# Attention sums carried from group to group: a vector add in SBUF, or an identity product into the accumulating bank

## The reference, cut to what matters

```python
alpha = einsum(h_src, a_src) + einsum(h_dst, a_dst) + sum(relu(edge_attr @ edge_W.T + edge_b) * h_dst)
alpha = where(alpha >= 0, alpha, 0.2 * alpha)
amax = segment_max(alpha, dst)
ex = exp(alpha - amax[dst])
denom = segment_sum(ex, dst)
out = segment_sum(h_src * (ex / denom[dst])[..., None], dst)
```

## Time and profile before

| | |
|---|---|
| median of 3 runs | 2690.42 us (2685.27 to 2691.62) |
| profiled execution | 2690.11 us, its span 2688.3 us |
| attention stage | about 1542 to 2216 us |
| busy in the whole span | TensorE 72%, VectorE 62%, GpSimd 46%, ScalarE 34% |
| mean granted TensorE clock | 0.87 |
| DMA | 366 MB, mean 136 GB/s |

### The profile page before, as it was taken

One profiled execution on the slowest core, in us unless ns is written; L12 is line 12 of the kernel. 1 busy time (PEld: TensorE's weight loads), 2 busy tenths in 40 slices (PEclk: granted clock), 3 DMA queues, 4 the chain that ended last, 5 costly groups with the idle time before them and its releaser, 6 DMA issues. The chain is left out here.

```text
span 2688.3 us, 41194 instructions
## 1 busy us (share of the span) xinstructions
PE 1935.6 (72%) x12513; PEld 1495.2 (56%) x12602; DVE 1661.8 (62%) x3351; ACT 908.4 (34%) x2284; POOL 1235.4 (46%) x1222
## 2 busy tenths in 40 slices
PE   3366666666279986599922478888888877969995
PEld 1244545445157765499921256666666652329994
DVE  8556555555157767655566779999999986021222
ACT  7333323333100002133312445555555543413331
POOL 0377777777710000255511377777777740002221
PEclk9678877776689998699966689999999998989997
DMA  2355544444478851522223155555555535001113
GB/s 78 106 181 201 188 165 169 171 162 166 145 284 287 293 190 65 169 72 72 71 87 103 43 173 162 159 161 158 162 163 159 163 90 188 18 2 36 36 38 112
DMA packets 192123, 366.13 MB, mean 136 GB/s; under 512 B 47573, under 2 KB 102632, under 8 KB 191525
## 3 DMA queue, kind: packets, MB, share of 16 engines
q1 hardware_dynamic: 135472, 207.05, 23.8%
q0 software_dynamic: 56160, 156.43, 18.5%
q10 hardware_dynamic: 274, 0.00, 0.0%
HBM read 232.23 MB, written 131.07 MB: 135 GB/s over the span
## 5 line engine op out<-in xcount | busy, mean ns | idle before, releaser
L1930 POOL DMA_INDIRECT att_rows<-hdram,top_ix x488 | 501.7, 1028 | 149.7 <-issue 145.7
L839 POOL DMA_INDIRECT mtab<-first_w,msgs_ix x308 | 309.0, 1003 | 94.0 <-issue 88.5
L708 PE MATMUL msgs_p_m<-nodes_n,msgs_hott 128*128 x976 | 319.8, 484 | 37.9 <-issue 30.7
L2000 PE MATMUL att_p_acc<-att_msg,att_hot 128*128 128x264 f32 x976 | 255.7, 407 | 78.3 <-ACT att_msg L2045 56.2
L708 PEld LDWEIGHTS msgs_p_m<-nodes_n,msgs_hott 128*128 128x128 f32 x976 | 223.7, 241 | 90.3 <-issue 53.4
L2000 PEld LDWEIGHTS att_p_acc<-att_msg,att_hot 128*128 128x128 f32 x976 | 180.9, 195 | 122.7 <-DVE att_msg L2167 57.3
L1141 POOL IOTA route_column<- 128x50 f32 (+1 forms) x2 | 0.3, 172 | 523.7 <-ACTq L1137 523.7
L1341 PE MATMUL exp_y<-exp_own,exp_ht 128*128 128x256 f32 x1032 | 239.0, 379 | 2.4 <-issue 2.4
L2030 ACT ACTIVATE att_enc<-att_p_z 128x1024 f32<-128x1024 f32 x122 | 125.0, 1024 | 301.3 <-PE att_p_z L1943 301.3
L839 POOL DMA_INDIRECT mtab<-msgs_rw,msgs_ix x180 | 181.8, 1010 | 72.8 <-issue 52.8
L1341 PEld LDWEIGHTS exp_y<-exp_own,exp_ht 128*128 128x128 f32 x1032 | 188.5, 190 | 24.7 <-issue 3.1
(11 more groups left out here) (389 smaller groups left out, 3997.9 us busy)
## 6 DMA issues: line engine op xcount, KB each, us to landing
first_w<-mtab SPq DMA_DIRECT2D x77, 520.0 KB, 4.8
etab<-msgs_et SPq DMA_DIRECT2D x122, 288.0 KB, 2.2
att_hz<-etab SPq DMA_DIRECT2D x122, 288.0 KB, 2.9
msgs_rw<-mtab SPq DMA_DIRECT2D x45, 520.0 KB, 4.7
first_w<-in_L_ffn_w SPq DMA_DIRECT2D x16, 512.0 KB, 4.7
ffn0x_w<-in_L_ffn_w SPq DMA_DIRECT2D x16, 512.0 KB
ffn_w<-in_L_ffn_Wd SPq DMA_DIRECT2D x8, 1024.0 KB, 11.8
att_rows<-hdram,top_ix POOLq DMA_INDIRECT x488, 3.0
```

Source lines behind the costliest of these rows:

```text
L708: last = T.matmul(p_m[g % 2][:, q, :], hott[g % 2][:, q, :], node, start=True, stop=True)
L839: nc.gpsimd.indirect_dma_start(mtab, bass.IndirectOffsetOnAxis(ap=ix[:, g, q:q + 1], axis=0), rw[g % RS][:, q, :], None).then_inc(s_free[g ...
L1930: nc.gpsimd.indirect_dma_start(rows[:, g % RS, q, :], None, hdram, bass.IndirectOffsetOnAxis(ap=ix1[:, g, q:q + 1], axis=0)).then_inc(s_ro ...
L2000: last = T.matmul(p_acc[g % 2][:, 0:HW], hot[g % 2][:, q, :], msg[g % 2][:, q, :], start=(q == 0), stop=(q == G - 1))
```

## The change

The running sum no longer goes through VectorE. `sums(g)` keeps its bank open after the four products and adds a fifth: the identity as weights and the tile `total` of group g-1 as moving side, so that the bank holds the group's sums plus the old total. ScalarE then copies the bank out twice: `pass_total(g)` copies it to `total`, scaled by `keep` for group g+1 (for the last group of a batch without scale, since VectorE's `fallen` multiplies it by `fall`, which also holds the change of a tile); and `keep_total(g)` copies it to `acc`. `gathered` is gone. `fallen` runs once per batch, at the end of a step with s % 4 = 3, ahead of `alphas`. `pass_total(s - 8)` stands in ScalarE's step behind `encodings(s + 1)`; `keep_total` keeps its place, for group s - 8 in place of s - 9. The semaphore `s_add` goes; `s_total` and `s_fallen` come.

```diff
--- before.py
+++ after.py
@@ -1888,9 +1888,9 @@
     p_top = a.ps("p_top", [P, 512])
     p_line, p_back, a_top, a_edge = (p_top[:, k * P:(k + 1) * P] for k in range(4))
     (s_z, s_enc, s_h, s_prod, s_red, s_adst, s_al, s_line, s_chain, s_rb, s_back, s_backc, s_top, s_new, s_fall, s_edge,
-     s_dif, s_ex, s_msg, s_wide, s_acc, s_add, s_go, s_weight, s_kept, s_node) = (a.sem(m) for m in (
+     s_dif, s_ex, s_msg, s_wide, s_acc, s_total, s_go, s_weight, s_kept, s_node, s_fallen) = (a.sem(m) for m in (
          "z", "enc", "h", "prod", "red", "adst", "al", "line", "chain", "rb", "back", "backc", "top", "new", "fall", "edge",
-         "dif", "ex", "msg", "wide", "acc", "add", "go", "weight", "kept", "node"))
+         "dif", "ex", "msg", "wide", "acc", "total", "go", "weight", "kept", "node", "fallen"))
     s_rows, s_hz, s_seg = ([a.sem(f"{m}{s}") for s in range(k)] for m, k in (("rows", RS), ("hz", SE), ("seg", 2)))
 
     def groups(t):
@@ -1995,10 +1995,16 @@
                 pe.wait_ge(s_wide, g + 1)
                 pe.wait_ge(s_weight, g + 1)
                 if g >= 2:
-                    pe.wait_ge(s_add, g - 1)
+                    pe.wait_ge(s_kept, g - 1)
                 for q in range(G):
                     last = T.matmul(p_acc[g % 2][:, 0:HW], hot[g % 2][:, q, :], msg[g % 2][:, q, :],
-                                    start=(q == 0), stop=(q == G - 1))
+                                    start=(q == 0), stop=(g == 0 and q == G - 1))
+                if g:
+                    if g % BG == 0:
+                        pe.wait_ge(s_fallen, g // BG)
+                    else:
+                        pe.wait_ge(s_total, g)
+                    last = T.matmul(p_acc[g % 2][:, 0:HW], cst["ident"][:], total[(g - 1) % 2][:], start=False, stop=True)
                 last.then_inc(s_acc, 1)
 
             encoders(0)
@@ -2060,12 +2066,20 @@
                 act.wait_ge(s_new, t + 1)
                 S.activation(fall[t % 2][:], fall[t % 2][:], ACT.Exp).then_inc(s_fall, 1)
 
+            def pass_total(g):
+                act.wait_ge(s_acc, g + 1)
+                if g + 1 < NG:
+                    if (g + 1) % BG:
+                        S.activation(total[g % 2][:], p_acc[g % 2][:, 0:HW], ACT.Copy,
+                                     scale=keep[:, g + 1:g + 2]).then_inc(s_total, 1)
+                    else:
+                        S.copy(total[g % 2][:], p_acc[g % 2][:, 0:HW]).then_inc(s_total, 1)
+
             def keep_total(g):
                 b = act.value_load(gb[0:1, g:g + 1], min_val=0, max_val=NT - 1)
-                act.wait_ge(s_add, g + 1)
                 if g:
                     act.wait_ge(s_kept, g)
-                S.copy(acc[:, bass.ds(b, 1), :].rearrange("p a c -> p (a c)"), total[g % 2][:]).then_inc(s_kept, 1)
+                S.copy(acc[:, bass.ds(b, 1), :].rearrange("p a c -> p (a c)"), p_acc[g % 2][:, 0:HW]).then_inc(s_kept, 1)
 
             def exponents(t):
                 w = len(groups(t)) * G
@@ -2080,6 +2094,8 @@
                 t, j = s // BG, s % BG
                 if s + 1 < NG:
                     encodings(s + 1)
+                if 0 <= s - LAG - 1 < NG:
+                    pass_total(s - LAG - 1)
                 if s + 2 < NG:
                     own_tile(s + 2)
                 if j == 0 and 0 < t <= NB:
@@ -2092,8 +2108,8 @@
                     weights(s - LAG)
                 if 0 < s - LAG + 1 < NG:
                     widen(s - LAG + 1)
-                if 0 <= s - LAG - 2 < NG:
-                    keep_total(s - LAG - 2)
+                if 0 <= s - LAG - 1 < NG:
+                    keep_total(s - LAG - 1)
             act.wait_ge(s_kept, NG)
 
         @block.vector
@@ -2168,26 +2184,15 @@
                                 rows[:, g % RS, :, 0:C].rearrange("p q (h d) -> p q h d", d=D),
                                 bc(ex[t % 2][:, j * G:(j + 1) * G, :], 3, D), ALU.mult).then_inc(s_msg, 1)
 
-            def gathered(g):
-                t, j = g // BG, g % BG
-                last, to = total[(g + 1) % 2], total[g % 2]
-                if g >= 2:
-                    dve.wait_ge(s_kept, g - 1)
-                if j == 0:
-                    dve.wait_ge(s_fall, t + 1)
-                    link(V.tensor_tensor(to[:].rearrange("p (h d) -> p h d", d=D + 1),
-                                         last[:].rearrange("p (h d) -> p h d", d=D + 1), bc(fall[t % 2][:], 2, D + 1), ALU.mult))
-                    dve.wait_ge(s_acc, g + 1)
-                    V.tensor_tensor(to[:], to[:], p_acc[g % 2][:, 0:HW], ALU.add).then_inc(s_add, 1)
-                else:
-                    dve.wait_ge(s_acc, g + 1)
-                    V.scalar_tensor_tensor(to[:], last[:], keep[:, g:g + 1], p_acc[g % 2][:, 0:HW], ALU.mult,
-                                           ALU.add).then_inc(s_add, 1)
-                dve.wait_ge(s_add, g + 1)
+            def fallen(t):
+                to = total[(t * BG - 1) % 2]
+                dve.wait_ge(s_fall, t + 1)
+                dve.wait_ge(s_total, t * BG)
+                V.tensor_tensor(to[:].rearrange("p (h d) -> p h d", d=D + 1), to[:].rearrange("p (h d) -> p h d", d=D + 1),
+                                bc(fall[t % 2][:], 2, D + 1), ALU.mult).then_inc(s_fallen, 1)
 
             same_windows()
             link(V.memset(tops[:, 0, :], -BIG))
-            link(V.memset(total[1][:], 0.0))
             for s in range(NG + LAG + 3):
                 t, j = s // BG, s % BG
                 if s < NG:
@@ -2200,8 +2205,8 @@
                     differences(t - 1)
                 if 0 <= s - LAG < NG:
                     messages(s - LAG)
-                if 0 <= s - LAG - 1 < NG:
-                    gathered(s - LAG - 1)
+                    if (s - LAG) % BG == 0 and s > LAG:
+                        fallen((s - LAG) // BG)
                 if s < NG and (j == BG - 1 or s == NG - 1):
                     alphas(t)
```

## The result

The changed kernel takes 2765.57 us (median of 4 runs, 2764.07 to 2767.94), the kernel before in the same comparison 2690.35: a ratio of 1.0284, 95% interval 1.0266 to 1.0302. It is slower by 75 us; the forecast was 2766.

What follows compares the result with a forecast made beforehand. The prediction took a ring of TensorE and ScalarE waiting for each other, not VectorE, as the bound; +66.2 us in the window, +2.4 before and +7.5 after, together +76 on 2690, gave 2766 us, range 2740 to 2800.

Steps and rivals of the forecast that it cites:

- the ring: Attention loop: TensorE's `p_z`, ScalarE's Relu, `own_tile`, `weights`, TensorE's sums, next `p_z`; 20.50 us per batch, growing to 23.76.
- TensorE's product: The fifth, identity product after each group's four, in every group but the first: 0.467 us, wholly in the ring.
- rival 4: On TensorE the fifth product's wait holds back its weight load: up to 46 us more, 2789 to 2812 us; chance 0.07.
- ScalarE's copy: `pass_total` between Relu and `own_tile`, in the ring: net 0.37 us for three groups of a batch, 0.28 for one.
- rival 3: ScalarE's idle time absorbs the copy, so only TensorE's term counts: about 2724 us; chance 0.04.
- Nothing for `keep_total` and `fallen`: `keep_total`, last in ScalarE's step, and `fallen`, once per batch on VectorE, fit in spare time and cost nothing.
- the last groups: The last eight groups, without Relus between, become a chain with sums about 3.2 us apart: +7.5 us.
- the half-clock steps: Four loop places with TensorE's clock at half level, counted as gone; if they stay, 7 us more or slightly above.
- rival 5: TensorE's longer gap before the sums drops its clock once per batch: 63 us more, 2829 us; chance 0.04.
- 66.2, 2.4 and 7.5: Added us for the 109 full-pipeline steps, the steps before that window, and the last eight groups; together +76.
- GpSimd is the bound: GpSimd's gathers, 5.33 us per group, set the mean step, so nothing moves: 2690 us; chance 0.03.
- the 22.6 us credited for the fourth step: Most that removing VectorE's excess in each batch's fourth step could save; at least 6.7 us of it clock falls.

Runs made afterwards that it cites:

- run 3: The changed kernel without the identity product, `pass_total` and `fallen`, so VectorE is relieved and nothing is added: 2679.71 us, ratio to before 0.9947.
- run 1: The changed kernel with `pass_total` moved on ScalarE from behind the Relu to behind `weights`: 2718.23 us, ratio to before 1.0097.
- run 2: The changed kernel without TensorE's identity product, whose two waits stand before the fourth product: 2711.81 us, ratio to before 1.0073.
- run 4: The changed kernel with `weights` moved on ScalarE from behind `own_tile` to ahead of the Relu: 2693.1 us, ratio to before 1.0008.
- run 9: The changed kernel with only VectorE's message product issued as two halves, `weights` left behind `own_tile`: 2762.98 us, ratio to before 1.0286.
- run 5: The kernel before with `weights` moved on ScalarE ahead of the Relu: 2689.76 us, ratio to before 1.0004.
- run 6: The changed kernel with `weights` ahead of the Relu and VectorE's message product issued as two halves: 2667.95 us, ratio to before 0.992.

## Why the prediction was right, and where it was not

*The bound.* Right that VectorE, at 92%, was not it. The three steps of a batch in which it did not come last showed that, and run 3 confirms it: with VectorE relieved and nothing added 11 us are gained, not 58. Right too that the ring sets the step of the changed kernel: runs 1, 2 and 4 take either part or the closing copy out of it and gain 47, 54 and 72 us, and run 9 shows that faster gathers give nothing there.

*TensorE's product.* Taken at 0.467 us, a little high, and all in the ring. The timeline shows 0.44, run 2 gives 0.445 per step. The weight load is hidden (rival 4 falls): in the timeline the product starts 1.86 us after the group's first, as `line` did before.

*ScalarE's copy.* Taken at 0.37 and 0.28 us net; the timeline shows 0.37 and 0.25, and run 1 gives 0.349 in the mean. Durations of 0.476 and 0.373 us against 0.471 and 0.380. The estimate worked out from the Trainium skill, "ScalarE: Activation LUTs", What ACT_TABLE_LOAD costs, 0.499 us for the scaled copy, was the worse one. That idle time absorbs it (rival 3) falls with run 1: nothing but the copy's place saves it.

*Nothing for `keep_total` and `fallen`.* Right; VectorE waits 68.7 us in 28 places for the copy before `fallen`, and only GpSimd waits for VectorE in return, which costs nothing there.

*The sum.* The ring was to grow to 23.76 us per batch; it is 5.97 + 5.79 + 6.01 + 5.87 = 23.64. The loop gave +63.1 for +66.2, the last groups +7.6 for +7.5: where no batch work comes between, their sums start 3.28 us apart behind the plain copy and 3.37 behind the scaled one (3.2 was forecast), each waiting for the copy of the one before. The TensorE clock, at 1.00 over the whole loop, did not fall once there: the half-clock steps went as assumed, and rival 5 did not come. That the forecast met the median to half a microsecond is partly luck. In the profiled executions the terms that it adds up, 66.2, 2.4 and 7.5, came to 63.1, 2.2 and 7.6, 3 us less, and the 4.9 us outside the stage, which it does not have, make up for it.

*What failed.* The step of the prediction that says what bounds the kernel before. It took the ring for the bound of the mean step, put the 0.83 us per batch between ring and real mean down to VectorE's lateness, late rows and four falls of the clock, and gave "GpSimd is the bound" 0.03. Run 5 shows that the ring did not set the mean: cut alone, it gave nothing. In ordinary batches VectorE's adds did not set it either, as run 3 shows (20.99 and 21.00 us). The ring gave three steps their length, and the rows, which GpSimd's stretched gathers brought late, lengthened the fourth. Of the 22.6 us credited for the fourth step 9.5 were the falls of the clock (at least 6.7 was forecast), and they alone went with VectorE's adds in run 3. The forecast did not suffer, since the new ring lies above GpSimd's pace and its length was added up by itself, but the expectation for run 3 did: 2667 us with the ring alone, 2680 measured. It also hid the better version. Of what was to show it, "GpSimd waiting for VectorE's products" appears only in gaps marked as issue of up to 1.1 us in place of 0.3, and in the stretched gathers; and TensorE's wait for `att_msg` in 82 groups of 110, with the wait for `copy_back` in 27 more.

What stays open: how much of the 4.9 us outside the stage belongs to the change. Most of it is spread: what lies before the first Relu of the loop and from the next stage's first operation on took 2016.8 us before and 2021.1 with the change, but in the ten other profiles it lies between 2013.8 and 2020.2, for kernels with and without the change. And why the clock falls in the loop in three of the four versions in which VectorE adds, and in none of the eight others.

## What to carry to other kernels

An engine's busy share does not tell whether work added to it is free: ScalarE was idle for almost half of the window and a copy of 0.37 us cost 0.35 per step, because it stood between a wait for TensorE and the operation TensorE waits for. Look for pairs of engines that wait for each other, follow the ring once round, and place added work outside of it, or first take the operation that closes the ring (here a copy of 0.25 us) ahead of the wait. Then compare the mean step with the pace of every engine that never waits: it may already be the next bound, and the gain ends there. But ask, too, whether anyone waits for what it makes, since an operation that is held back from inside looks busy (run 1). And where the clock differs between two profiles, compare the steps without its falls.

## What the runs showed of the hardware

A gather issued by GpSimd takes 0.949 us, and up to 1.99 when it starts during a VectorE product with both inputs in SBUF: it ended 0.82 us after that product's end in all 91 cases of the changed kernel. The 52 gathers that were already running when such a product began kept their 0.95, and a product with one input in a bank did nothing to it. Cutting the product of 1.22 us in two brought the longest gather from 1.70 to 1.47 us and the mean from 1.030 to 0.981 (runs 4 and 6), and the kernel from 2693.1 to 2668.0 us. ScalarE copies 128x264 in 0.388 us from a bank and in 0.412 from SBUF, both to `acc`; from a bank to `total` it takes 0.373, and with a per-partition scale 0.476. In the loop of the kernel before, TensorE's granted clock was at half level in four stretches, and a batch with one took 2.4 us longer.
